# First attention: maximum steps whose halves share a burst taken by one VectorE instruction over two banks

## The reference, cut to what matters

```python
def _L0_attn_ref(x, ...):               # x: 4 x 1024 x 256, 16 heads of 16
    q = q.astype(jnp.float32) * scale
    attn = jnp.einsum('bqhd,bkhd->bhqk', q, k)
    attn = jax.nn.softmax(attn, axis=-1)          # softmax over 1024 keys
    out = jnp.einsum('bhqk,bkhd->bqhd', attn, v)
    ...
```

## Time and profile before

| | us |
|---|---|
| median of 3 runs (lowest, highest) | 1914.5 (1914.3 to 1917.1) |
| the profiled execution | 1909.4 |
| span of its trace | 1907.4 |
| the stage of the first attention with its maxima | about 131 to 790 of the span |

### The profile page before, as it was taken

One profiled execution on the slowest core, in us unless ns is written; L12 is line 12 of the kernel. 1 busy time (PEld: TensorE's weight loads), 2 busy tenths in 40 slices (PEclk: granted clock), 3 DMA queues, 4 the chain that ended last, 5 costly groups with the idle time before them and its releaser, 6 DMA issues. The chain is left out here.

```text
span 1907.4 us, 34604 instructions
## 1 busy us (share of the span) xinstructions
PE 1795.9 (94%) x12690; PEld 1170.9 (61%) x12690; DVE 1429.7 (75%) x2814; ACT 1117.3 (59%) x2212; POOL 528.6 (28%) x686
## 2 busy tenths in 40 slices
PE   8989999999999999799999989999999987999994
PEld 4545444444444444388888865555555566999994
DVE  7879999999999999367677655466666554766665
ACT  4645888888888888622333214446463632655555
POOL 5760000233000001032223212212525243444444
PEclk9986999999999999899999988999999998999997
DMA  4883744565434502023444255546666334655555
GB/s 170 280 260 53 124 79 96 131 144 122 86 57 73 83 28 85 20 76 111 153 143 147 89 188 120 137 100 156 153 154 156 97 107 147 150 144 144 145 115 196
DMA packets 146600, 239.18 MB, mean 125 GB/s; under 512 B 25830, under 2 KB 81159, under 8 KB 146449
## 3 DMA queue, kind: packets, MB, share of 16 engines
q1 hardware_dynamic: 113312, 171.48, 36.8%
q0 software_dynamic: 17024, 34.25, 7.0%
q10 hardware_dynamic: 16112, 31.46, 4.5%
HBM read 137.49 MB, written 96.60 MB: 123 GB/s over the span
## 5 line engine op out<-in xcount | busy, mean ns | idle before, releaser
L994 DVE TENSOR_REDUCE b_mx<-b_PM 128x1 f32<-128x512 f32 x1024 | 621.0, 679 | 17.9 <-PE b_PM L848 17.5
L970 ACT ACTIVATE b_probs<-b_PS 128x512 f32<-128x512 f32 x1000 | 523.9, 606 | 69.1 <-PE b_PS L902 53.8
L848 PE MATMUL b_PM<-b_kst,b_qst 48*128 48x512 f32 x888 | 280.9, 430 | 0.0
L2919 ACT ACTIVATE d_probs<-d_PS 128x512 f32<-128x512 f32 (+3 forms) x384 | 166.5, 496 | 183.2 <-PE d_PS L2822 182.5
L902 PE MATMUL b_PS<-b_qst,b_kst 50*128 50x512 f32 x744 | 256.9, 436 | 2.1 <-issue 0.2
L2958 DVE TENSOR_REDUCE d_mx<-d_PM 128x2 f32<-128x1024 f32 (+1 forms) x192 | 179.9, 950 | 101.5 <-PE d_PM L2774 59.3
L902 PEld LDWEIGHTS b_PS<-b_qst,b_kst 50*128 50x128 f32 x744 | 120.4, 184 | 163.4 <-ACT b_probs L970 147.4
L2874 POOL TENSOR_SCALAR_AFFINE_SELECT d_probs<-d_probs 128x128 f32<-128x128 f32 x256 | 74.6, 305 | 268.1 <-ACT d_probs L2919 263.4
L790 POOL CAST b_mhalves<-b_maxima 128x16 fp32r<-128x16 f32 x32 | 6.3, 197 | 505.3 <-DVE b_maxima L1003 505.3
L848 PEld LDWEIGHTS b_PM<-b_kst,b_qst 48*128 48x128 f32 x888 | 142.0, 184 | 5.4
L874 PE MATMUL b_PO<-b_probs,x_v 128*32 128x384 f32 (+2 forms) x2048 | 145.2, 390 | 0.0
(11 more groups left out here) (318 smaller groups left out, 3753.9 us busy)
## 6 DMA issues: line engine op xcount, KB each, us to landing
halves<-a_parts SPq DMA_DIRECT2D x7, 2048.0 KB, 8.7
qk<-c_halves ACTq DMA_DIRECT2D x7, 2048.0 KB
w_w<-L_ffn_fc1T SPq DMA_DIRECT2D x12, 1024.0 KB, 5.0
w_w<-L_ffn_fc2T SPq DMA_DIRECT2D x12, 1024.0 KB, 6.3
b_qst<-halves SPq DMA_DIRECT2D x72, 128.0 KB, 4.4
b_kst<-halves SPq DMA_DIRECT2D x72, 128.0 KB, 7.6
d_qst<-qk SPq DMA_DIRECT2D x36, 256.0 KB, 5.2
d_kst<-qk SPq DMA_DIRECT2D x36, 256.0 KB, 7.4
```

What stands on the lines that cost most here:

```text
L848: mm = pe.matmul(PM[n % MBANKS][:], qst[buf][at, p, first:first + P], kst[buf][at, p, kh * BLK:(kh + 1) * BLK], start=True, stop=True)
L970: act.activation(probs[:, s % RING], score_bank(g, s)[:], ACT.Exp).then_inc(exped, 1)
L994: dve.tensor_reduce(mx[:, half, (r * PAIRS0 + p) * TPH + t, kh:kh + 1], PM[n % MBANKS][:], AX.X, ALU.max)\
L2919: act.activation(probs[:, s % RING, 0:w], PS[bank(s)][:, 0:w], ACT.Exp).then_inc(exped, 1)
```

## The change

For a maximum step whose two products lie in the same burst, VectorE waits for both and takes them with one reduction of 1024 columns over two neighbouring banks, which then counts `max_taken` up by two. The step's other column of `mx` holds -3e38 from a memset at the start. A step whose products fall into two bursts is taken by halves, as before; the 24 steps ahead of all units are taken whole. The four banks `PM0` to `PM3` become one tensor of four banks. `join_maxima` moves behind the second product of the next half's first step. TensorE's order and its waits are unchanged.

By the places of the units, the steps that start at units 0, 4, 6, 10, 12, 16, 18, 24, 26 and 30 of a half are taken whole, and those at 2, 8, 14, 20, 22 and 28 by halves.

```diff
+    def whole(n):
+        s = (n - AHEAD * HALVES) // HALVES * HALVES
+        return s < 0 or place(s % UNITS) // SBANKS == place(s % UNITS + 1) // SBANKS
...
-        PM = [a.ps(f"PM{i}", [P, BLK]) for i in range(MBANKS)]
+        PM = a.ps("PM", [P, MBANKS, BLK])
...
-                    mm = pe.matmul(PM[n % MBANKS][:], qst[buf][at, p, first:first + P],
+                    mm = pe.matmul(PM[:, n % MBANKS], qst[buf][at, p, first:first + P],
...
             dve.sem_inc(max_taken, MBANKS)
+            dve.memset(mx[:], -3.0e38).then_inc(mx_set, 1)
+            dve.wait_ge(mx_set, 1)
 
             def take(n):
                 x, kh = n // HALVES % STEPS, n % HALVES
                 half, t, p, r = step_at(x)
-                dve.wait_ge(max_scores, n + 1)
-                dve.tensor_reduce(mx[:, half, (r * PAIRS0 + p) * TPH + t, kh:kh + 1], PM[n % MBANKS][:], AX.X, ALU.max)\
-                   .then_inc(max_taken, 1)
+                out = mx[:, half, (r * PAIRS0 + p) * TPH + t]
+                if not whole(n):
+                    dve.wait_ge(max_scores, n + 1)
+                    dve.tensor_reduce(out[:, kh:kh + 1], PM[:, n % MBANKS], AX.X, ALU.max).then_inc(max_taken, 1)
+                elif kh == 0:
+                    dve.wait_ge(max_scores, n + HALVES)
+                    both = PM[:, n % MBANKS:n % MBANKS + HALVES].rearrange("p h n -> p (h n)")
+                    dve.tensor_reduce(out[:, 0:1], both, AX.X, ALU.max).then_inc(max_taken, HALVES)
...
-                if n % HALF_MAXIMA == 0 and n > 0:
+                if n % HALF_MAXIMA == HALVES - 1 and n > HALVES:
                     join_maxima(n // HALF_MAXIMA - 1)
```

More of the change, by code:

```diff
@@ L681, in phase_attention0 @@
         PT = PS[TURN_PLACES[0] % SBANKS][:, 0:P]
-        WIDE = [*PM, PS[bank(WIDE_FROM - 2)], PS[bank(WIDE_FROM - 1)], PS[TURN_PLACES[0] % SBANKS]]
+        WIDE = [*(PM[:, i] for i in range(MBANKS)),
+                *(PS[b][:] for b in (bank(WIDE_FROM - 2), bank(WIDE_FROM - 1), TURN_PLACES[0] % SBANKS))]
         def score_bank(g, s):
-            return WIDE[(s - WIDE_FROM) % WBANKS] if wide(g, s) else PS[bank(s)]
+            return WIDE[(s - WIDE_FROM) % WBANKS] if wide(g, s) else PS[bank(s)][:]
         setup, ones_made, ones_set = a.sem("setup"), a.sem("ones_made"), a.sem("ones_set")
-        max_scores, max_taken, max_made = a.sem("max_scores"), a.sem("max_taken"), a.sem("max_made")
+        max_scores, max_taken, max_made, mx_set = (a.sem(n) for n in ("max_scores", "max_taken", "max_made", "mx_set"))
         m_high, m_cut, m_turned, m_copied, rows_in = (
@@ L901, in score @@
                 at = slice(r * ROWS0, r * ROWS0 + KM)
-                pe.matmul(score_bank(g, s)[:], kst[g % BUFS][at, p, kt * P:(kt + 1) * P],
+                pe.matmul(score_bank(g, s), kst[g % BUFS][at, p, kt * P:(kt + 1) * P],
                           qst[g % BUFS][at, p, half * BLK:(half + 1) * BLK], start=True, stop=True).then_inc(scores, 1)
@@ L969, in unit @@
                     act.wait_ge(pv_done, g * ROUNDS + s // G0 + 1)
-                act.activation(probs[:, s % RING], score_bank(g, s)[:], ACT.Exp).then_inc(exped, 1)
+                act.activation(probs[:, s % RING], score_bank(g, s), ACT.Exp).then_inc(exped, 1)
             copy_rows(0)
```

## The result

| | before | after |
|---|---|---|
| median us (lowest to highest, runs) | 1915.8 (1914.3 to 1920.9, 4) | 1954.6 (1953.5 to 1956.7, 4) |
| the profiled execution | 1909.4 | 1956.7 |
| start of the first maximum product to the weight load of unit 32 of the last group, us of the trace | 640.5 | 678.2 |
| a half of a group, median of the 29 at full clock | 19.66 | 20.78 |

The ratio is 1.0199, with a 95% interval of 1.0177 to 1.0221: the change is slower, by 39 us. The stage alone is 37.7 us longer, between the same two instructions of the two traces. The two profiled executions differ by 47 us. Of the rest, 8.9 us lie behind that instruction, in later stages that the change doesn't touch and that took 1135 to 1146 us in the ten traces of this case, and 0.6 ahead of the first product.

A forecast was written before the change was run, and what follows sets the result against it. TensorE was taken as the bound, with VectorE about 2% short of it. Halves 28.8 plus prologue and early units 2.5 gave +31.3 us on 1909.4, 1940.7; with the median 5.1 us higher, 1945, range 1920 to 1956.

The forecast's parts named there:

- a third load is free up to about 0.47 us into a burst: In TensorE's bursts, a third weight load costs nothing until about 0.47 us; all beyond is added to TensorE's time.
- the release moves from 0.73 to 1.27 us: The load of product n + 4 may come 1.27 us after the start of reduction n, not 0.73.
- four places in a half pay: Bursts 26-28 and 32-34 lose 0.27 us each, 12-14 loses 0.41, 18-20 loses 0.07.
- A half: Half of a group: 0.27 + 0.27 + 0.41 + 0.07 - 0.06 = +0.96 us, so 19.64 becomes 20.6.
- The prologue: First 48 products: two pairs need 2.53 us where four narrow reductions took 2.39; first score product +2.0 us.
- The predicted chain: From the first join through cast, transpose, copy and DMAs to the first score product: follows the later join, +2.0 us.
- The first and last halves: Stage's ends: 0.6 for the rest of the first half plus 0.5 at clock 0.5, and 0.35 for the last's beginning.
- Two wide ones at the head of a burst: A pair first in its burst delays the next burst's second load: 0.1 us, but nothing where that burst is already held up.
- The clock: Rival: TensorE's gaps let its clock fall to 0.5 in the stage, some 45 us on top, 1990; chance 0.07.
- VectorE is the limit: Rival: VectorE sets the pace, each of 334 pairs returns 0.056 us, 18.7 us in all, 1896; chance 0.09.

The follow-up runs named there:

- count_one: The changed kernel, but a wide reduction adds one to max_taken, not two, and can carry its own wait: 1945.9 us, ratio 1.0161.
- two_first: Against the kernel before, wide reductions only for the steps of units 0 and 26 of each half: 1926.7 us, ratio 1.0056.

## Why the prediction was right, and where its sizes were off
It said 1945 with a range of 1920 to 1956, slower; measured were 1954.6. The mechanism was right for the halves, which are nearly all of the loss: TensorE sets the pace, a third load is free up to about 0.47 us into a burst, the release moves from 0.73 to 1.27 us, and four places in a half pay. For the prologue the path was wrong. Of the 9.6 us between forecast and measurement 6.4 lie in the stage; the others are the median of the kernel before (1915.8, not 1914.5), rounding, and 1.1 us outside the stage.

- **A half.** 0.96 us were predicted, 1.12 measured, 4.8 us over 29 halves. The mis-sized term is the start of the wide reduction: it was put at 0.03 to 0.04 us behind its product, and comes 0.07 later than a narrow one. The diff had it in plain sight, `then_inc(max_taken, HALVES)` in place of 1, and the rows of the second attention could not show it, since that kernel counts by one. Without the detail the half was 20.63 (`count_one`), 0.97 over the kernel before.
- **The prologue.** +2.0 us up to the first score product were predicted, 3.2 measured. In after, the pairs go by 2.61 us for two:

```profile
133.58 2.36 DVE L1008 TENSOR_REDUCE b_mx<-b_PM 128x1 f32<-128x1024 f32 x2 [1.38 <-PE b_PM L855]
136.18 2.36 DVE L1008 TENSOR_REDUCE b_mx<-b_PM 128x1 f32<-128x1024 f32 x2 [0.25 <-PE b_PM L855]
...
155.53 0.18 DVE L1016 TENSOR_REDUCE b_maxima<-b_mx 128x16 f32<-128x32 f32 x1
```
  The join stands 23.3 us behind the first product, 2.7 later than before; 2.53 us for two pairs had been the estimate, and the difference is again the start of the wide one. With the count by one the trace has 2.54 (132.93 to 135.47), and the join 2.2 us later. But the chain behind the join, by which the prediction went, is not what the first score product waits for. TensorE's order has all 48 maximum products ahead of it, and they wait for VectorE's releases up to the last pair. The weight loads in before:

```profile
159.00 0.28 PEld L848 LDWEIGHTS b_PM<-x_k,x_q 48*128 48x128 f32 x1 [0.32 <-DVE b_mx L994]
159.19 0.31 PEld L902 LDWEIGHTS b_PS<-x_q,x_k 50*128 50x128 f32 x1
```
  and in after:

```profile
162.42 0.50 PEld L855 LDWEIGHTS b_PM<-x_k,x_q 48*128 48x128 f32 x2 [0.97 <-DVE b_mx L1008]
163.01 0.33 PEld L909 LDWEIGHTS b_PS<-x_q,x_k 50*128 50x128 f32 x1
```
  The last of the 48 loads 27.3 us behind the first product in before and 30.3 in after, and the score product follows 0.2 and 0.4 us later. The DMAs of the first rows had ended at 26.5 and 28.9. So the 3.2 us are what the 48 products take longer, 2.61 in place of 2.39 us for four, with the first pair starting 0.5 us later. The predicted chain gave 2.0 us and comes near this by luck, as what delays it, the pace of the pairs, delays the 48 products too.
- **The first and last halves.** Predicted 0.6 + 0.5 for the first; measured 1.0. Predicted 0.35 for the last; measured 0.8, since the long burst of its units 0 to 2 belongs to it and I had left that out.
- **Two wide ones at the head of a burst** were put at 0.1 us each if they stood alone, and cost 0.2 each (`two_first`). The forecast didn't need it.
- Sum: 32.6 + 3.2 + 1.0 + 0.8 = 37.7 us of the stage (from unrounded terms), against 31.3 predicted. Of the difference of 6.4 us the separate wait explains 5.4 (`count_one`, +32.3 in the stage).
- **The clock** rival did not come: PEclk is 1.00 from 180 to 780 us of the trace of after. From 131 to 170 us it is 0.50, as before.
- **"VectorE is the limit"** was given 0.09. The halved reductions settle it: 0.05 us a half.

Two notes of the Trainium skill bear on this. The Vector Engine (DVE) Microarchitecture Reference, section 5.2, has some 75 ns as the fixed cost of an instruction after queue overlap. The trace of after agrees nearly: 1.14 us from start to start for 1024 columns against 2 x 0.598, so 0.056 us saved by a pair. VectorE: DVE Perf Modes, "Rules for kernel authors", advises for chained operations to minimise their count, not the semaphores. The count was cut here, to 695 reductions in place of 1024, though they are not chained by their data. VectorE's own time fell, as the note would have it, and the kernel lost 2%, a part of it by the semaphore. So in this case the measurement decides against the count as a measure for the kernel's time, because VectorE's instructions were not on the path and the moment of their release was.

## What to carry to other kernels
Before two instructions are merged, ask when the buffers they read come free, not only what the instruction costs: with four banks in the ring, a reader that takes two at a time gives the first one back half a microsecond later, and the writer's queue stands still for it with all that lies behind. Whether that costs is a matter of place, and can be read off the trace beforehand: the start of the load that waits, and how late it may come before its burst gets longer. An engine that is 99% busy need not be the limit; halve what it reads once and see.

## What the runs showed of the hardware that was not expected
- An increment by two split the wait off: the trace has a separate wait ahead of nearly every wide reduction, and these started 0.092 us after the signal, the others 0.024. In this kernel 0.07 us at that place was worth 5 us.
- TensorE's listed busy time grew from 19.56 to 20.71 us a half with the same matmuls. Their ends are modelled, and the listed times cover the waits between them.
- How late a load may come depends on its place in the burst, by an estimate from these bursts: a third one up to about 0.47 us (at 0.76 the burst lasts 1.97, at 0.81 it lasts 2.02, against 1.69), a second one up to about 0.24 (at 0.45 it lasts 1.89, against 1.69).
